# Fetching one or two tiles per three turns row by row from SyncE and ScalarE, instead of by GpSimd gathers

## The reference, cut to what matters

```python
h   = s @ lin1_ws ...                      # one row of 160 floats per node
hid = silu(edge_scalars @ fc_w1 * _inv(R)) # (E, 64), first layer only
w   = hid @ fc_w2 * _inv(FC_HID)           # (E, 224)
es  = h_s[edge_src]; ev = h_v[edge_src]    # the fetch of rows by source node
m_s1 = w1 * es * e0                        # and four more products
agg_s = jax.ops.segment_sum(mid_s, edge_dst, num_segments=n) * inv_nn
```

## Time and profile before

| what | us |
|---|---|
| median of three runs | 2017.59 |
| the profiled execution | 2016.04 |
| its span | 2014.2 |
| first gather of the first layer, last one starts | 37.4, 1008.6 |
| first gather of the second layer, last one starts | 1055.1, 1991.1 |
| GpSimd busy, TensorE busy, VectorE busy, ScalarE busy | 1459.9, 1695.3, 1277.7, 174.8 |

### The profile page before, as it was taken

One profiled execution on the slowest core, in us unless ns is written; L12 is line 12 of the kernel. 1 busy time (PEld: TensorE's weight loads), 2 busy tenths in 40 slices (PEclk: granted clock), 3 DMA queues, 4 the chain that ended last, 5 costly groups with the idle time before them and its releaser, 6 DMA issues.

```text
span 2014.2 us, 41903 instructions
## 1 busy us (share of the span) xinstructions
PE 1695.3 (84%) x15596; PEld 1443.5 (72%) x15596; DVE 1277.7 (63%) x2725; ACT 174.8 (9%) x392; POOL 1459.9 (72%) x1558
## 2 busy tenths in 40 slices
PE   6989898989898989898958877878787878778786
PEld 4767676767676767676737877878787878778786
DVE  6787878787878877878875545444444545454443
ACT  5100000000000000000050000000000000000000
POOL 2777777777777777777737777777777777777774
PEclk9999999989999989989968989899998989899998
DMA  6333333333333333333322222222222223222223
GB/s 234 104 104 89 100 98 100 98 100 97 99 99 99 98 99 99 98 99 99 100 60 70 72 68 70 69 71 68 71 68 70 69 70 71 68 71 69 70 68 83
DMA packets 106120, 176.80 MB, mean 88 GB/s; under 512 B 27328, under 2 KB 73104, under 8 KB 105952
## 3 DMA queue, kind: packets, MB, share of 16 engines
q0 software_dynamic: 73200, 125.03, 25.5%
q1 hardware_dynamic: 30560, 49.88, 7.6%
q10 hardware_dynamic: 2320, 1.44, 0.2%
HBM read 170.10 MB, written 6.14 MB: 87 GB/s over the span
## 4 chain that ended last, share of the span: by engine, by line
POOL 69%; issue 22%; PE 4%; DVE 2%; DMA 1%; ACT 1%; POOLq 1%; DVEq 0%; ACTq 0%
POOL g L594 69%; PE sums L847 1%; PE w_ps L858 1%; DMA g<-node_table,src 1%; PE sums L868 1%; PE w_ps L457 1%; ACT H L268 0%; POOLq L589 0%; PE sums L858 0%; PE w_ps L812 0%; DMA node_table<-H 0%; PE w_ps L1020 0%; DVE work L721 0%; DMA ident_sb<-ident_dram 0%; PE sums L843 0%
## 5 line engine op out<-in xcount | busy, mean ns | idle before, releaser
L594 POOL DMA_INDIRECT g<-node_table,src x1525 | 1445.2, 948 | 494.8 <-issue 462.4
L847 PE MATMUL sums<-g,sel 128*128 128x160 f32 x1612 | 294.7, 344 | 178.7 <-DMA g<-node_table,src 177.4
L847 PEld LDWEIGHTS sums<-g,sel 128*128 128x128 f32 x1612 | 270.1, 223 | 195.9 <-DMA g<-node_table,src 139.9
L858 PE MATMUL w_ps<-H,work 128*128 128x160 f32 x2900 | 405.2, 300 | 2.5 <-DVE work L688 2.5
L858 PEld LDWEIGHTS w_ps<-H,work 128*128 128x128 f32 x2900 | 398.0, 191 | 2.7 <-DVE work L688 2.7
L721 DVE TENSOR_TENSOR work<-w_ps,g 128x384 f32<-128x384 f32 (+3 forms) x693 | 299.0, 459 | 114.5 <-DMA g<-node_table,src 67.7
L740 DVE STREAM_TRANSPOSE turned<-sums 128x160 f32<-128x160 f32 x232 | 80.1, 345 | 440.3 <-PE sums L868 303.5
L812 PE MATMUL w_ps<-fc_sb,work 64*128 64x224 f32 x1612 | 241.8, 398 | 89.2 <-DVE work L715 87.0
L843 PEld LDWEIGHTS sums<-work,sel 128*32 128x32 f32 x6448 | 202.6, 114 | 115.1 <-issue 78.0
L812 PEld LDWEIGHTS w_ps<-fc_sb,work 64*128 64x128 f32 x1612 | 173.2, 200 | 139.5 <-DVE work L715 120.4
L671 DVE TENSOR_TENSOR sel<-mixed,sh 128x896 f32<-128x896 f32 x232 | 251.7, 1085 | 28.9
(11 more groups left out here) (81 smaller groups left out, 536.3 us busy)
## 6 DMA issues: line engine op xcount, KB each, us to landing
feat<-edge_feat_dram SPq DMA_DIRECT2D x60, 512.0 KB
g<-node_table,src POOLq DMA_INDIRECT x1525, 2.6
named<-src_rows_dram SPq DMA_DIRECT2D x30, 128.0 KB, 3.0
X<-x_dram SPq DMA_DIRECT2D x5, 400.0 KB, 6.9
node_table<-H SPq DMA_DIRECT2D x5, 400.0 KB, 2.7
named<-src_rows_dram SPq DMA_DIRECT2D x30, 64.0 KB
sh<-edge_sh_dram SPq DMA_DIRECT2D x1, 1624.0 KB, 8.8
out_dram<-X SPq DMA_DIRECT2D x4, 240.0 KB, 3.3
```

Of the source, the lines that this page charges most:

```text
L594: nc.gpsimd.indirect_dma_start(out=g[:, u, j, :], out_offset=None, in_=table[layer], in_offset=bass.IndirectOffsetOnAxis(ap=src[:, at:at + ...
L847: last = nc.tensor.matmul(sums[:, o % 2, 0:D], sel[:, o % 2, j, :], g[:, o % UNROLL, j, :], **first_last)
L858: last = nc.tensor.matmul(found_at[:, i, 0:D], match[layer][:, i, t, :], H[:, t, :], start=(t == 0), stop=(t == NT - 1))
```

## The change

Turns are now taken in periods of three (`PERIOD`). 29 turns are 2 turns ahead (`LEAD`) and 9 periods. `stages` writes the 2 turns ahead, then a hardware loop over 8 periods with a body of three turns, then the last period. `passes` counts passes from 1 instead of turns in steps of 29.

`g` gets two spare tiles. In turn p = 0 of each period, tile 6 of group 3 lies in the first spare tile; in the second layer, in turn p = 1, it lies in the second. GpSimd doesn't gather these tiles: 9 gathers fewer in the first layer, 18 fewer in the second. In their place an engine reads eight node numbers at a time from a row of the new input `src_by_row` into registers and issues one DMA of one row (640 bytes) for each:

- SyncE fetches the first spare tile in both layers, over the three turns from when it is free to when it is used: 48, 48 and 32 rows (`PARTS`), the first quarter of each part ahead of the turn's loads of `named` and `feat` half 0, the rest between these and `feat` half 1.
- ScalarE fetches the second spare tile in the second layer: 12 rows at the end of each of ten groups' stages, then 8, then none (`SHARES[1]`).

VectorE (first layer, before the second chunk of products) or TensorE (second layer, before tile 6) waits for `row_landed`.

```diff
+PERIOD = 3
+LEAD = ITERS % PERIOD
+PERIODS = ITERS // PERIOD
+ROW_TILES = (1, 2)
+PARTS = (48, 48, 32)
+SHARES = ((0, 12, 12, 12) + (12,) * 4 + (12, 12, 12, 8), (12,) * 8 + (12, 12, 8, 0))
+AT_ONCE = 8
...
-        g = sb("g", [P, UNROLL, TILES, D])
+        g = sb("g", [P, UNROLL * TILES + 2, D])
...
-            def stages(eng, q, stage, last):
-                for s in range(UNROLL):
-                    stage(q, 0, s, s)
-                with eng.Fori(1, ITERS - 1) as it:
+            def stages(eng, r, stage, last):
+                q = eng.snap(ITERS * r)
+                e = eng.snap(PERIODS * r + 0) - 1
+                for it in range(LEAD):
                     f = eng.snap(q + it)
                     for o in range(UNROLL):
-                        stage(f, it, o, None)
+                        stage(f, it, o, UNROLL * it + o, it - LEAD, e, -1)
+                with eng.Fori(0, PERIODS - 1) as k:
+                    e = eng.snap(PERIODS * r + k)
+                    for p in range(PERIOD):
+                        it = eng.snap(PERIOD * k + (LEAD + p))
+                        f = eng.snap(q + it)
+                        for o in range(UNROLL):
+                            stage(f, it, o, None, p, e, k)
...
+            def slot(p, u, j):
+                if u == UNROLL - 1 and j >= CHUNKS[1][0] and 0 <= p < ROW_TILES[layer]:
+                    n = j - CHUNKS[1][0]
+                    return (UNROLL * TILES - 3 + 2 * n) if p == 0 else (UNROLL * TILES - 2 + n)
+                return u * TILES + j
+            def by_row_at(p, u, j):
+                return j == TILES - 1 and u == UNROLL - 1 and 0 <= p < ROW_TILES[layer]
+            def fetch_rows(eng, which, i, a, b):
+                to = slot(i, UNROLL - 1, TILES - 1)
+                for c in range(a, b, AT_ONCE):
+                    d = min(c + AT_ONCE, b)
+                    _, nodes = nc.values_load_multi_w_load_instructions(by_row[i][0:1, c:d], engines=(which,), min_val=0, max_val=N - 1,
+                                                                        skip_runtime_bounds_check_because=LOAD_CHECK)
+                    for k, node in zip(range(c, d), nodes):
+                        eng.dma_start(g[k:k + 1, to, :], table[layer][bass.ds(node, 1), :]).then_inc(row_landed[i], 16)
+            def begin_rows(eng, i, f, e, again):
+                if again:
+                    eng.wait_ge(prod_done if own_weights else agg_done, eng.snap((2 if own_weights else 1) * UNROLL * f))
+                eng.wait_ge(by_row_in[layer][i], eng.snap(16 * e + 16))
...
+            def sync_turn(sp, f, it, part, e, k):
+                a, b = sum(PARTS[:part]), sum(PARTS[:part + 1])
+                some = a + (b - a) // 4
+                if part == 0:
+                    begin_rows(sp, 0, f, e, not isinstance(k, int))
+                fetch_rows(sp, mybir.EngineType.SP, 0, a, some)
+                more_rows(sp, f, it)
+                more_feat(sp, f, it, 0)
+                fetch_rows(sp, mybir.EngineType.SP, 0, some, b)
+                more_feat(sp, f, it, 1)
+                if part == PERIOD - 1:
+                    load_by_row(sp, 0, k + 1)
...
-                    tiles = min(tiles_of(UNROLL * it + u), by_pool[u])
+                    p = (it - LEAD) % PERIOD if it >= LEAD else -1
+                    tiles = min(tiles_of(UNROLL * it + u), by_pool[u] - by_row_at(p, u, TILES - 1))
...
+                def row_part(f, it, o, s, p, e, k):
+                    if ROW_TILES[layer] < 2 or o >= UNROLL or p < -1 or (p == PERIOD - 1 and s is not None):
+                        return
+                    part = (p + 1) % PERIOD
...
+                    fetch_rows(act, mybir.EngineType.Activation, 1, a, b)
...
+                    elif by_row_at(p, u, TILES - 1):
+                        dve.wait_ge(row_landed[p], 16 * P * e + 16 * P)
...
+                        if not own_weights and by_row_at(p, o % UNROLL, j):
+                            pe.wait_ge(row_landed[p], 16 * P * e + 16 * P)
```

More of the change, by code:

```diff
@@ L83, with build @@
 PICKED = ((2,), (0, 2))
-def build(nc, x, node_vec, src_idx, src_rows0, src_rows1, node_id, dst_idx, edge_sh, edge_feat, ident, iota, lin_sc, lin_sc_scale,
+PERIOD = 3
+LEAD = ITERS % PERIOD
+PERIODS = ITERS // PERIOD
+assert LEAD == PERIOD - 1
+ROW_TILES = (1, 2)
+PARTS = (48, 48, 32)
+SHARES = ((0, 12, 12, 12) + (12,) * 4 + (12, 12, 12, 8), (12,) * 8 + (12, 12, 8, 0))
+AT_ONCE = 8
+assert all(sum(n) == P for n in (PARTS, *SHARES))
+LOAD_CHECK = "a transfer with a computed address is checked against the table's end"
+def build(nc, x, node_vec, src_idx, src_rows0, src_rows1, src_by_row, node_id, dst_idx, edge_sh, edge_feat, ident, iota, lin_sc, lin_sc_scale,
           fc1, fc2, big0, big0_scale, l1_pair, l1_pair_scale, l1_out, l1_out_scale, out):
@@ L130, in build @@
         node_id_sb = sb("node_id_sb", [P, NT])
+        by_row = [sb(f"by_row{i}", [1, P], I32) for i in range(2)]
         named = sb("named", [P, max(map(len, PICKED)), P], I32)
@@ L182, in build @@
         named_in = [sem(f"named_in{l}") for l in range(2)]
+        by_row_in = [[sem(f"by_row_in{l}{i}") for i in range(2)] for l in range(2)]
         big0_in = sem("big0_in")
@@ L490, in edge_layer @@
             named_read = sem(L + "named_read")
+            row_landed = [sem(L + f"row_landed{i}") for i in range(2)]
             match_done = sem(L + "match_done")
@@ L536, in sync_picks @@
[L536 to L545, removed]
-                    sp.sem_inc(pass_left, 1)
@@ new lines, in stages @@
+                with eng.Fori(0, PERIODS - 1) as k:
[5 more added lines that the diff above has]
+                            stage(f, it, o, None, p, e, k)
+                e = eng.snap(PERIODS * r + (PERIODS - 1))
+                for p in range(PERIOD):
+                    it = ITERS - PERIOD + p
+                    f = eng.snap(q + it)
+                    for s in range(UNROLL * it, UNROLL * (it + 1) if p < PERIOD - 1 else last):
+                        stage(f, it, s - UNROLL * it, s, p, e, PERIODS - 1)
@@ L653, in stage @@
                         copy(f, 1 if o >= UNROLL else 0)
-                with passes(act) as q:
-                    stages(act, q, stage, GROUPS + 2)
+                    row_part(f, it, o, s, p, e, k)
+                if ROW_TILES[layer] == 2:
+                    load_by_row(act, 1, 0)
+                with passes(act) as r:
+                    stages(act, r, stage, GROUPS + 2)
+                    if ROW_TILES[layer] == 2:
+                        rows_end(act, 1, r)
             def vector(dve):
@@ L704, in products @@
                     w = w_ps[:, h, 0:n, :]
-                    rows = g[:, u, a:b, :]
+                    at = [slot(p, u, j) for j in range(a, b)]
+                    rows = g[:, at[0]:at[-1] + 1:at[1] - at[0] if n > 1 else 1, :]
                     to = prod[:, o % 2, a:b, :]
```

134 lines of the change are left out of this document (78 added, 56 removed).

## The result

The changed kernel takes 1984.51 us in the median of four runs (1984.08 to 1984.93), the kernel before 2017.49 us. The ratio is 0.9836 (95% interval 0.9819 to 0.9853), or 33.0 us less. The forecast was 1985 us. The profiled execution took 1984.93 us, its span is 1983.0 us.

A forecast was written before the change was run, and what follows sets the result against it. GpSimd issuing gathers back to back was taken as the bound: span 2014.2 - 33.75 = 1980.45, plus 1.84 around it, 1.55 to the median, 1 for loops and 0.5 for traffic: 1985 us; likeliest 1981 to 1990, eight in ten up to 2015.

The forecast's parts named there:

- Step 1: GpSimd: 27 gathers removed at 1.25 us each gain 33.75 us, as the other engines have room.
- Step 2: SyncE: a row costs 0.53 us (0.2 to 1.1); 128 rows fit below 0.74 us, or 0.70 in layer two.
- Step 3: ScalarE, second layer: 12 rows take about 6 us per stage; no cost up to about 0.7 us a row.
- Step 4: DMA queues: 3456 rows of 2 to 32 packets, probably near the upper count, delay gathers 0 to 1 us in all.
- Step 5: TensorE, VectorE, ScalarE loops: longer three-turn bodies may stall for code, at most some 5.5 us each; 1 us taken overall.
- The sum: Whole kernel: span less removed gathers, plus time around the span, median offset, loops and traffic; 1985 us.
- The 0.5 us for traffic and 1 us for the loops: Whole kernel: allowances added to 1983.8 us for small row packets and longer loop bodies.
- B: TensorE and VectorE stall at the first layer's branch back; 1990 to 2022 us, about 2000; chance 0.14.
- D: Small row packets slow the gathers' own issue; one percent costs 19 us, giving 2004 us; chance 0.05.
- C: Row DMAs too slow, SyncE becomes the bound from 0.74 us a row (0.70 in layer two); 2160 to 2600 us; chance 0.15.
- E: No effect because another bound stands close behind, excluded unless TensorE's clock falls; chance 0.03.

The follow-up runs named there:

- f1: Changed kernel's three-turn loops, but no rows fetched one by one and all 1525 tiles gathered by GpSimd; 2016.99 us, 0.9998 of the kernel before.
- f2: Changed kernel with all 3456 row DMAs, but all 1525 tiles still gathered and used, the rows unread; 2020.36 us, 0.9999 of the kernel before.
- g_sync_only: Changed kernel without ScalarE's rows, GpSimd gathering those nine tiles again (1507 gathers); 1995.49 us, 0.9889 of the kernel before.
- f4_act_both: Changed kernel with ScalarE fetching a second spare tile in the first layer too (1489 gathers); 2083.78 us, 1.0316 of the kernel before.
- g_two_values: Changed kernel with two node numbers per register load in place of eight; 2403.37 us, 1.186 of the kernel before.

## Why the prediction was right, point by point

- *Step 1, the gathers removed: right.* 27 x 1.25 = 33.75 us were forecast, 33.0 us came in the medians, 32.9 us between the gathers of the two traces. f1 and f2 show that neither the loops nor the rows add or take anything by themselves, g_sync_only that nine gathers are worth 11.0 us.
- *Step 2, SyncE: the price of a row was right, its parts were not, and that was luck.* A row was put at 0.53 us and cost 0.53. Without its share of the register load it was put at 0.46 us and takes 0.41: the DMA's issue was shorter than that to 128 partitions (0.228 against 0.333 us), the gaps were longer (0.12 against 0.05 us). Its share of the load was put at 0.07 us and is 0.12, because a load of eight values is longer than one of one (0.72 against 0.53 us). The time around the 128 rows was put at 5 us and measured as 10 to 13 us in the slower kernels. So the point from which SyncE decides is 0.70 us, not 0.74, in the first layer, and ScalarE's in the second is 0.64, not 0.70. At 0.53 and 0.54 us that changed nothing, but the room was 0.17 and 0.10 us a row where 0.21 and 0.17 had been counted.
- *Step 3, ScalarE: right for the second layer.* 12 rows were put at 6 us and take 6.4, and TensorE never waits there for one of ScalarE's copies. f4_act_both shows how much hung on the length of ScalarE's pauses: the same 12 rows in the first layer cost 99 us.
- *Step 4, traffic: the low end held.* A row is two packets, not 32: q10 has 1152 packets of 640 bytes and 1162 of 4 bytes more than before. The DMA share went from 0.38 and 0.29 to 0.39 and 0.30. The Trainium skill's rule of sixteen pieces ("DMA: Bandwidth & Descriptors", section "Why a DMA increments its semaphore by 16 and not by 1") does not hold in the count of packets for this DMA: the measurement decides.
- *Step 5, the loops: the mechanism was there, its price was nil.* q8 went from 15 to 106 packets, in the first layer over and over and in the second not, as the page "Runtime: NRT & Kernel Launch", section "Instruction fetch mechanics" of the Trainium skill, would have it for a body that doesn't fit; the trace agrees with the fetches, and f1_loops_only at 0.9998 shows that the stalls it names do not reach the path here. The forecast had taken 1 us.
- *The sum came within 0.8 us (1985.3 before rounding), and part of that is luck.* The span was to be 1980.45 + 1.5 = 1981.95 us and is 1983.0, 1.05 us more. From the span to the median the forecast added 1.84 + 1.55 us; measured are 1.93 (1984.93 - 1983.0) and -0.42 (1984.51 - 1984.93), 1.9 us less. How far one profiled execution lies from its median does not carry over from one kernel to the next.
- *The 0.5 us for traffic and 1 us for the loops* are close to the 1.56 us lost after layer one. The stretch is 1.47 us longer already in f1_loops_only, where TensorE's clock is low at the same place; a stall for code was not seen there, and traffic is not needed for it.
- *Rivals.* B and D are refuted by f1 and f2. C did not occur, and g_two_values shows that it does at 0.81 us a row; by the estimate above it would begin 0.1 to 0.2 us above what a row costs, on ScalarE perhaps earlier. E did not occur: the gain came, and the granted clock was 0.92 in both profiled executions.

## What to carry to other kernels

Where one queue issues back to back all through and the others have measured room, taking instructions from it is worth their pitch, to within a few per cent; what has to be worked out is not the gain but whether the engine that takes over has the time. There two questions are separate: is its time enough (rows per period times their pitch, register loads and the 10 us around them included), and how long is one batch against the shortest interval in which that engine must answer someone. The second one failed first in f4_act_both: 6.4 us in front of a silu that was due after 5 us cost ten times what the rows brought.

## What the runs showed of the hardware that had not been expected

- The time of a register load did not grow from two to eight values: 0.50 us for one, 0.73 for two, 0.72 for eight, 1.16 for sixteen on SyncE.
- Issuing a DMA of one row of 640 bytes took 228 ns on SyncE, one to 128 partitions 333 ns (364 in the changed kernel); it left two packets in its queue.
- On ScalarE the first row DMA after a register load took 0.46 us and the others 0.22; on SyncE 0.26 and 0.23.
- Loading code seven times as often (1.74 MB in place of 0.25 MB on q8) cost no measurable time.
- Where TensorE and the small instructions of other engines are held up (kernel before at 2930.8 us) and the gathers are not the chain, 3456 more row DMAs cost 8.8%, and nothing where the gathers are.
